# Softplus as one ScalarE activation, a regrouped first stretch, and the first state sum placed ahead of two TensorE steps

## What is computed

```
h   = layernorm(x) * g + b                      # ln1, after a plain layernorm
xz  = rmsnorm(h) @ in_proj_w ; xi, z = split(xz)
xc  = silu(conv4(xi) + conv_b)
dbc = xc @ x_proj_w                             # 64 columns for delta, 16 B, 16 C
delta = softplus(dbc[:, :64] @ dt_proj_w + dt_proj_b)
h_t = exp(delta * A) * h_(t-1) + delta * xc * B     # 256 features x 16 states
y   = (sum over the 16 states of h_t * C + D * xc) * silu(z)
h   = h + y @ out_proj_w
x   = x + h ; x = x + relu(ln2(x) @ w1 + b1) @ w2 + b2
```

## Time and profile before

| | us |
|---|---|
| median of 3 runs | 1562.26 (1561.81 to 1565.87) |
| profiled execution, its own time | 1565.17 |
| its span, first to last instruction | 1563.4 |
| first scan of unit 0 in passes 0, 1, 2, 3, 4, 5 starts at | 52.25, 126.08, 207.66, 294.69, 377.60, 459.25 |
| last PE product of the first half ends about | 789 |

### The profile page before, as it was taken

The page is one execution under the profiler, slowest core; times in us unless marked ns, Lnnn a source line. Parts: engine busy times, 40 slices in busy tenths (PEclk is TensorE's granted clock), DMA queues, the critical chain, the costliest instruction groups (busy, mean ns, idle before and its releaser), DMA issues.

```text
span 1563.4 us, 17435 instructions
## 1 busy us (share of the span) xinstructions
PE 1379.8 (88%) x5582; PEld 670.7 (43%) x5582; DVE 1155.6 (74%) x1842; ACT 890.2 (57%) x1525; POOL 662.2 (42%) x394
## 2 busy tenths in 40 slices
PE   6525879999999999899957989999999999999998
PEld 2202444536364545455432324354544444444444
DVE  5888888989989897880259877686877777776325
ACT  6565758586867765532211564656565655655633
POOL 2486968788888876741424121313022112100000
PEclk8756989999999999999985999999999999999999
DMA  6524160616161524300245442314343432330045
GB/s 208 192 79 162 58 205 30 229 43 215 56 214 58 181 77 137 105 28 14 68 103 131 81 106 55 98 51 99 69 96 70 95 77 64 81 69 2 29 137 173
DMA packets 93803, 158.05 MB, mean 101 GB/s; under 512 B 8608, under 2 KB 74720, under 8 KB 90592
## 3 DMA queue, kind: packets, MB, share of 16 engines
q1 hardware_dynamic: 93712, 156.94, 34.7%
HBM read 110.91 MB, written 46.01 MB: 100 GB/s over the span
## 4 chain that ended last, share of the span: by engine, by line
PE 49%; DVE 18%; issue 14%; POOL 12%; ACT 4%; DMA 2%; SPq 0%; POOLq 0%; ACTq 0%; DVEq 0%
PE psum L1152 12%; PE psum L2138 8%; PE psum L2072 7%; PE psum L2046 6%; PE psum L2061 5%; POOL hb L1083 5%; DVE mx L1535 4%; DVE psum L608 4%; PE psum L2016 4%; PE psum L1204 2%; DVE middle L580 1%; DVE hb L611 1%; PE psum L1177 1%; POOL x_front L1064 1%; POOL front L1056 1%
## 5 line engine op out<-in xcount | busy, mean ns | idle before, releaser
L1786 ACT ACTIVATE pw<-psum 128x512 f32<-128x512 f32 x512 | 302.1, 598 | 275.6 <-PE psum L2061 272.5
L1535 DVE TENSOR_REDUCE mx<-psum 128x1 f32<-128x512 f32 x512 | 343.7, 685 | 153.8 <-PE psum L2046 152.6
L1083 POOL TENSOR_TENSOR hb<-ddb,bcb 128x1024 f32<-128x1024 f32 x127 | 296.6, 2360 | 73.3 <-DVE middle L580 51.1
L608 DVE TENSOR_TENSOR_SCAN psum<-psum,hb 128x512 f32<-128x512 f32 x224 | 262.0, 1215 | 54.6 <-POOL hb L1083 27.3
L2046 PE MATMUL psum<-kp,qp 96*128 96x512 bf16 x512 | 203.7, 403 | 31.6 <-DVE mx L1535 21.8
L874 ACT ACTIVATE psum<-ddb,A_neg 128x512 f32<-128x512 f32 x256 | 165.3, 681 | 83.6 <-DVE hb L611 66.6
L2061 PE MATMUL psum<-qp,kp 99*128 99x512 bf16 x512 | 197.3, 387 | 5.0 <-ACT pw L1786 4.3
L1954 POOL TENSOR_TENSOR rstd<-rstd,neg_half 128x4 f32<-128x4 f32 x16 | 16.3, 1018 | 413.7 <-DVE rstd L1520 413.7
L611 DVE TENSOR_TENSOR hb<-psum,bcb 128x1024 f32<-128x1024 f32 x112 | 137.1, 1224 | 3.9
L2072 PE MATMUL psum<-pw,v_sb 128*32 128x512 f32 x1024 | 125.8, 609 | 0.5 <-ACT pw L1786 0.5
L1152 PE MATMUL psum<-back,w 128*128 128x512 f32 x256 | 114.1, 599 | 2.1 <-ACT back L890 1.9
(11 more groups left out here) (235 smaller groups left out, 2180.5 us busy)
## 6 DMA issues: line engine op xcount, KB each, us to landing
ddb<-dd SPq DMA_DIRECT2D x64, 512.0 KB, 6.2
bcb<-bc SPq DMA_DIRECT2D x32, 512.0 KB, 6.7
parts<-parts_sb SPq DMA_DIRECT2D x96, 128.0 KB
qp<-parts SPq DMA_DIRECT2D x32, 256.0 KB, 7.6
dd<-dd_out SPq DMA_DIRECT2D x7, 1024.0 KB, 4.8
kp<-parts SPq DMA_DIRECT2D x16, 384.0 KB, 4.6
x_back<-x_dram SPq DMA_DIRECT2D x9, 512.0 KB, 8.5
xh_back<-xh SPq DMA_DIRECT2D x8, 512.0 KB, 3.8
```

The costliest lines, as they stand in the source:

```text
L608: e.tensor_tensor_scan(to[:, g, :], a[:, g, :], h[:, g, :], 0.0, ALU.mult, ALU.add).then_inc(scan_ok, 1)
L1083: e.tensor_tensor(hb[n % NHB], ddb[k % NSLOT][:, 1:2, :].to_broadcast([P, 2, L]), bcb[q][:, 0, :, :], ALU.mult).then_inc(bx_ok, 2 if n == ...
L1535: used.up(e.tensor_reduce(mx[u % 2][:, n:n + 1], score_bank(used.n), AXIS.X, ALU.max))
L1786: e.activation(pw[n % NPW], bank(5 + n % 2), ACT.Exp, scale=HD ** -0.5).then_inc(exp_ok, 1)
```

## The change

1. Softplus is one activation: `mid_delta(b, f)` on ACT reads the product `dt` from PSUM and writes delta, twice per batch. Abs, Relu, Exp, Identity and Ln on ACT, `mid_soft` on DVE and the first tensor_tensor of `mid_du` on POOL are gone, and with them the tile `middle1` and the waits on `part_ok`, `lin_ok` and `d_ok`.
2. The convolution uses the weights as they are (`conv_half` is gone), and silu has no scale of 2.
3. In the opening stretch silu is one activation too, the table loads are placed by small activations on one column (`table`), the moments of batch 1 are taken before `first_sum(0)`, and the steps of ACT for batch 1 are cut into halves that stand between the steps of batch 0. PE's filling products between `mid_dt(0)` and `front(1)` are 5 in place of 9, and the wait on `relu_ok` is gone.
4. On PE `sums(i, 0)` stands before `back_turn` and `mid_xp`.
5. On ACT `gate_i(i-2, 0)` stands before `back_apply`, `gate_i(i-2, 1)` behind it (both were behind `decay` of unit 5), and `back_turned` stands behind `decay` of unit 5 (it was behind that of unit 6).

The diff, cut:

```diff
@@ DVE, opening stretch
             def front_moments(b):
                 e.wait_ge(x_in[b % 2], 16 * (b // 2 + 1))
-                if b > 0:
+                if b == 1:
+                    e.wait_ge(f_rstd, 1)
+                elif b > 1:
                     e.wait_ge(xn_ok, b)
...
-            def first_relu(f):
+            def first_delta(f):
+
                 ring_out(e, "dt", 0, f)
-                e.tensor_scalar(feat(mid1)[:, f, :], ring("dt", 0, f), col("dt_b", f), 0.0, ALU.add, ALU.max).then_inc(relu_ok, 1)
...
+                e.wait_ge(xc_ok if f else xc_half, 1)
+                e.tensor_tensor(dd_out[:, f, 1, :], dd_out[:, f, 0, :], xc[0][:, f, :], ALU.mult).then_inc(du_ok if f else du_half, 1)
...
-            def mid_soft(b):
-
-                e.wait_ge(lin_ok, b)
-                e.scalar_tensor_tensor(feat(mid0), dd_out[:, :, 1, :], 1.0, feat(mid0), ALU.subtract, ALU.subtract).then_inc(part_ok, 1)
-                e.wait_ge(part_ok, 2 * b + 1)
-                e.tensor_tensor(mid1, mid1, mid0, ALU.subtract).then_inc(part_ok, 1)
...
@@ ACT
+            def first_x(f):
                 e.wait_ge(conv_ok, f + 1)
...
+                e.activation(xc[0][:, f, :], feat(mid0)[:, f, :], ACT.Silu).then_inc(xc_ok if f else xc_half, 1)
+
+            def table(fn):
+
+                e.activation(bg_nb[1][:, 0:1], neg_half[:, 0:1], fn)
...
+            def mid_delta(b, f):
+
+                ring_done(e, "dt", b, f)
                 if b == 1:
                     e.wait_ge(dd_half, 16)
...
+                if b > 0:
+                    e.wait_ge(dd_sent, 16 * b)
+                e.activation(dd_out[:, f, 0, :], ring("dt", b, f), ACT.Softplus, bias=col("dt_b", f)).then_inc(r_act, 1)
...
@@ ACT, opening stretch
             e.wait_ge(set_pool, 2)
-            mid_xi(0)
-            front_apply(1)
+            table(ACT.Silu)
+            mid_xi(0, (0,))
+            front_apply(1, (0, 1))
+            mid_xi(0, (1,))
+            front_apply(1, (2, 3))
             for f in range(NF):
-                first_th(f)
-            mid_z(0)
-            mid_tz(0)
+                first_x(f)
+            silu_z(0)
+            table(ACT.Softplus)
             mid_dbc(0)
+            front_square(1, (0, 1))
+            mid_delta(0, 0)
+            front_square(1, (2, 3))
+            mid_delta(0, 1)
             front_norm(1)
...
@@ ACT, pass
                         silu_x(i + 1)
+                    if u == 3 and gate:
+                        gate_i(i - 2, 0)
                     if u == 3 and back:
                         back_apply(i - 1)
-                    if u == 4 and gate:
-                        gate_i(i - 2, 0)
+                    if u == 3 and gate:
                         gate_i(i - 2, 1)
-                    if u == 5 and back:
+                    if u == 4 and back:
                         back_turned(i - 1)
...
                     if u == 8 and mid:
-                        mid_dt(i + 1)
+                        for f in range(NF):
+                            mid_delta(i + 1, f)
...
@@ POOL
             def mid_du(b):
-                e.wait_ge(part_ok, 2 * b + 2)
-                e.wait_ge(soft_ok, b + 1)
-                e.tensor_tensor(dd_out[:, :, 0, :], dd_out[:, :, 0, :], feat(mid1), ALU.add).then_inc(d_ok, 1)
-                e.wait_ge(d_ok, b + 1)
+                ring_out(e, "dt", b, 1)
...
@@ PE
-            stay_warm(9)
-            e.wait_ge(relu_ok, NF)
+            stay_warm(5)
             front(1)
...
+                if s:
+                    sums(i, 0)
                 if back:
                     back_turn(i - 1)
                 if mid:
                     mid_xp(i + 1)
-                if s:
-                    sums(i, 0)
```

More of the change, by code:

```diff
@@ L251, in build @@
         T0, T1 = (sb1(f"front{i}", NT * D) for i in range(2))
-        mid0, mid1 = (sb1(f"middle{i}", NT * D) for i in range(2))
+        mid0 = sb1("middle", NT * D)
         first.close()
@@ L716, in dve_first @@
                         front_moments(i + 2)
-                    if u == 10 and mid:
-                        mid_soft(i + 1)
                     if u == 11 and s:
@@ L800, in front_turned, with mid_xi @@
                     e.activation(feat(T1)[:, f, :], ring("fturn", b, f), ACT.Copy, scale=col("rms_w", f)).then_inc(r_act, 1)
-            def mid_xi(b):
-                for f in range(NF):
+            def mid_xi(b, parts=range(NF)):
+                for f in parts:
                     ring_done(e, "xi", b, f)
@@ L806, in mid_xi @@
                         e.wait_ge(conv_ok, 2 * (b - 1) + f + 1)
[L807 to L810 removed]
+                        e.wait_ge(xc_ok, b)
+                    e.activation(feat(mid0)[:, f, :], ring("xi", b, f), ACT.Identity, scale=col("conv_w", f * TAPS + TAPS - 1),
+                                 bias=col("conv_w", 8 + f)).then_inc(tap_ok, 1)
                     e.activation(xi_pad[:, f, TAPS - 1:], ring("xi", b, f), ACT.Copy).then_inc(r_act, 1)
[L813 to L822 removed]
             def silu_z(b):
@@ L836, in silu_x @@
                     e.wait_ge(du_ok, b - 1)
-                e.activation(xc[b % 2], feat(mid0), ACT.Silu, scale=2.0).then_inc(xc_ok, 1)
+                e.activation(xc[b % 2], feat(mid0), ACT.Silu).then_inc(xc_ok, 1)
             def mid_dbc(b):
@@ L843, in mid_dbc @@
                 e.activation(dbc[0:NR, :], ring("xp", b, 0)[0:NR, :], ACT.Copy).then_inc(r_act, 1)
-            def mid_dt(b):
-                for f in range(NF):
-                    ring_done(e, "dt", b, f)
-                    e.activation(feat(mid0)[:, f, :], ring("dt", b, f), ACT.Abs, bias=col("dt_b", f))
-                    e.activation(feat(mid1)[:, f, :], ring("dt", b, f), ACT.Relu, bias=col("dt_b", f)).then_inc(r_act, 1)
-            def mid_soft(b):
-                ring_out(e, "dt", b, 1)
-                own.up(e.activation(mid0, mid0, ACT.Exp, scale=-1.0))
-                e.wait_ge(own.sem, own.n)
-                e.wait_ge(dd_sent, 16 * b)
+            def mid_delta(b, f):
+                ring_done(e, "dt", b, f)
                 if b == 1:
                     e.wait_ge(dd_half, 16)
-                e.activation(dd_out[:, :, 1, :], feat(mid0), ACT.Identity, bias=1.0).then_inc(lin_ok, 1)
-                e.wait_ge(lin_ok, b)
-                e.wait_ge(xc_ok, b + 1)
-                e.activation(dd_out[:, :, 0, :], dd_out[:, :, 1, :], ACT.Ln).then_inc(soft_ok, 1)
+                if b > 0:
+                    e.wait_ge(dd_sent, 16 * b)
+                e.activation(dd_out[:, f, 0, :], ring("dt", b, f), ACT.Softplus, bias=col("dt_b", f)).then_inc(r_act, 1)
             def decay(b, u):
@@ L998, in act_first @@
                         back_relu(i - 1, 7)
-                    if u == 9 and mid:
-                        mid_soft(i + 1)
                     if u == 10 and front:
@@ L1030, in front_power @@
                 e.wait_ge(f_var, b + 1)
+                if b == 1:
+                    e.wait_ge(xn_ok, 1)
                 own.up(e.tensor_scalar(f_rs[:, 0, :].unsqueeze(2), f_mv[:, :, 1:2], EPS, None, ALU.add))
@@ L1123, in pool_first @@
                         front_scale(i + 2)
-                    elif u == 9 and mid:
-                        e.wait_ge(part_ok, 2 * i + 4)
                     if u == 12 and front:
```

120 lines of the change are left out of this document (24 added, 96 removed).

## The result

The median went from 1563.49 us (4 runs, 1561.81 to 1565.87) to 1547.43 us (4 runs, 1545.98 to 1549.06): 16.1 us less, ratio 0.9896 with a 95% interval of 0.9877 to 0.9916. The range of 1531 to 1552 holds it; the forecast of 1540 was 7 us too low. The profiled execution took 1546.26 us (span 1544.5), 18.9 less than the one of before. So 3.2 of the 7 us are a miss of the sum (22.1 against 18.9).

A forecast was written before the change was run, and what follows sets the result against it. PE was taken to bound the kernel from pass 2 on. Opening 3.5, pass 0 6.6, pass 1 5.6 and passes 2 to 6 6.4 sum to 22.1 us off 1565.17, median forecast 1540, range 1531 to 1552.

The forecast's parts named there:

- Softplus: On ACT, one 128x512 activation from PSUM with a bias, twice per batch: 0.67 us each, taken from a similar activation.
- Passes 0 and 1: Removed POOL and DVE steps and waits win 6.6 us in pass 0 and 5.6 in pass 1 (bounds 3.5 and 7.2).
- Passes 2 to 6, pass 4's mechanism: On PE, 2.8 us won before c=0 is given back by c=5; pass 4 keeps 0.41 less 0.15.
- Passes 2, 3 and 6, the cause: PE stood later against DVE in these passes, so they give more: 1.9, 1.5 and 2.4 us.
- only a rival that could take time away: PE's clock falls in new short gaps before c=3 and c=5, or parts cancel: 0 to 5 us won; chance 0.04.
- The opening, 3.5: Before the first decay: du sent 4.7 us earlier but sharing DMA with B and C loads, 3.5 us won, bounds 1.3 to 6.
- the mark I had set for it: Sign of being wrong in the opening stretch: first decay not earlier by 2 us; it was expected near 47.5.
- The second rival: DMA holds the opening at 1.3, pass 1 keeps 3.5, passes 2 to 6 give 4: 15.4 us, 1547; chance 0.16.
- Table switches: On ACT, each switch costs a load of 1.28 us with the next activation at once, no drain, in every sum.
- the third rival: A table switch holds ACT 1.28 us longer in passes 1 to 6, 7.7 in all: total 14.4, 1548; chance 0.05.
- The first rival: PE's gap in passes 2 to 6 is really won, 16 in place of 6.4: total 31.7 us, 1530.5; chance 0.14.
- The fourth rival: DVE sets every pass, each of seven giving 4.6 us and more: 46 and over, 1516; chance 0.04.

The follow-up runs named there:

- experiment 3: Kernel before plus dummy PE matmuls between the two transposes of back_turn, passes 2 to 7: six gave 1570.52 us, three gave 1558.86 us.
- experiment 4: Changed kernel with Exp in place of Softplus in batches 1 to 7, so no table loads around it: 1543.15 us, ratio 0.9854.
- both ACT edits: Changed kernel with relus of c=0 and c=1 ahead of unit 8's decay, softplus ahead of unit 9's, front_apply behind unit 10's: 1532.41 us, ratio 0.9794.

## Why the prediction was right, and where it was wrong

- **Softplus** was put at 0.67 and takes 0.69 (ACT at 33.64 in the timeline after). Right.
- **Passes 0 and 1**: 6.6 and 5.6 forecast, 6.76 and 5.15 measured, with the waits where they were put. In pass 1 the new wait before the scan of unit 10 is 2.69 and not 1.5 to 1.7; the 0.5 that it comes out short lies within the bounds.
- **Passes 2 to 6, pass 4's mechanism**: the gain at c=0 given back before c=3 and c=5, both by ACT. Right in both places; c=5 starts 44.19 us behind the sum of group 3 of the pass before, and it stood at 43.79 before (419.0 less 375.21). The pass keeps 0.02. I had 81.2 for a pass, it takes 81.63: the wait of 0.41 in front of the last sum is gone, but nothing is won by it, since c=5 is 0.4 later.
- **Passes 2, 3 and 6, the cause**: the sizes 1.9, 1.5 and 2.4 are near the measured 1.76, 1.29 and 2.17, but I said that PE was "later against DVE". It was later because its clock fell behind the 2.85 us gap, as the filled gap shows (experiment 3). In my text the clock was only a rival that could take time away. The sum came near all the same, since it took PE's lateness from the rows, whatever had made it; that no new fall would follow the new waits was assumed and not argued. The projection's duration, 3.62 at 568.21 in pass 6 against 1.93 at 404.55 in pass 4, stood in the trace of before and would have told.
- **The opening, 3.5**: this step failed, and the mark I had set for it (not earlier by 2 us) says so: 0.73. I had seen that B and C stand in front, moved du's sending by 4.7 us, and then let it land in 4.9 "and somewhat more". B and C moved by 0.64 and not by 1.3, so du left 3.94 earlier, and it took 8.3 us to land, 3.5 more than before. The 0.73 lies outside the term's own bounds (1.3 to 6) and is no larger than what the first decay differs by among profiles of the same opening. The Trainium skill (DMA: Bandwidth & Descriptors, "Queues, rings and completion order") says that each DMA engine takes the descriptors of one issuing engine's ring in their order; 4 x 512 KB ahead of du are then paid first. The traces agree: 8.3 to 9.1 us behind them in six profiles, 2.8 to 4.0 ahead of them in four. The second rival, with its 1.3 for "everything waits for the B and C loads", was nearer here; its 15.4 is near the 16.1 of the medians, though by luck: it has other numbers for the passes.
- **Table switches**: 1.28 us, the activation behind at once, 401.68 to 402.98. The drain that the Trainium skill adds (ScalarE: Activation LUTs, "What ACT_TABLE_LOAD costs") is not there in the rows; the third rival falls. The price of a switch on the path, 1.2 us a pass in passes 3 to 6, is measured by experiment 4.
- **The first rival**, 31.7 us from a gap really won, was false for this change; the kernel with both ACT edits has it, 32 us.
- **The fourth rival**, DVE in every pass, does not add up as written: seven passes of 4.6 with the 3.5 and 6.6 in front of them make 42 and not 46. It did not come near either way.
- **The second half** only moved: 18.68 us in pass 7, 18.9 at the end.

## What to carry to other kernels

When work is moved into a wait, follow the ring of buffers on: the time won must still be there at the next places that wait for a buffer, and the engine that frees them must not do it behind an instruction tied to a third engine; here an early softplus won 1.3 us a pass, two early relus nothing, and both together 3.1. In the trace, compare the durations of the same matmul right behind each idle gap before putting a late engine down to its neighbours. A transfer that others wait for is sent ahead of bulk loads on the same queue, but first look at who else waits for what is held back. And a gain of under 1 us at one mark, read from one trace each, says little: compare the mark in the traces of all kernels that share the code before it.

## What the runs showed of the hardware

- The same idle gap of PE is followed by the lower clock (granted 0.50) in some passes and not in others of one execution: 2.85 us in passes 2, 3 and 6 and not in 4 and 5 of the kernel before, 2.89 in pass 5 and not in 4 of the one with early relus. It costs 1.3 to 3 us. Waits of 1.62 and 0.99 were followed by none in passes 3 to 6. What decides it was not settled.
- Filling the gap of 2.85 with 2.7 us of dummy products kept the clock at 1.00 in passes 3 to 6 and made the kernel 4.5 us faster.
- A 512 KB store took 2.8 to 4.0 us to land ahead of the B and C loads on the same queue (four profiles) and 8.3 to 9.1 directly behind these 4 x 512 KB (six profiles); sent 5 to 7 us behind them, as before, 3.1 to 5.7.
- Softplus reads 128x512 from PSUM with a bias in 0.69 us, as fast as relu (0.67 to 0.69). The switch of table in front of it takes 1.28 us.
